# The experts' tiles written out for TensorE, both passes in one block, and semaphores cleared by ranges

## What is computed

```python
x = x + _L0_xattn_ref(_layernorm(x, axis=-1), ctx_1024, ctx_1024)
x = x + _L0_ffn_ref(_layernorm(x, axis=-1), L0_ffn_gate_w, L0_ffn_w_gate, L0_ffn_w_up, L0_ffn_w_down)
x = x + _L1_xattn_ref(_layernorm(x, axis=-1), ctx_1024, L1_xattn_Wq, L1_xattn_Wk, L1_xattn_Wv, L1_xattn_Wo)
x = x + _L1_ffn_ref(_layernorm(x, axis=-1), ...)

# _L0_ffn_ref
topk_w, topk_ids = jax.lax.top_k(scores, TOP_K)          # 8 of 64 experts a token
topk_w = topk_w / (topk_w.sum(axis=-1, keepdims=True) + 1e-20)
sorted_tokens = x[sort_idx // TOP_K]
g = jax.lax.ragged_dot(sorted_tokens, jnp.swapaxes(w_gate, 1, 2), group_sizes)
u = jax.lax.ragged_dot(sorted_tokens, jnp.swapaxes(w_up, 1, 2), group_sizes)
h = jax.nn.silu(g) * u
out = jax.lax.ragged_dot(h, jnp.swapaxes(w_down, 1, 2), group_sizes)
y = (unsorted.reshape(B * S, TOP_K, D) * topk_w[..., None]).sum(axis=1)
```

## Time and profile before

| | us |
|---|---|
| median of 3 runs | 1179.89 (1178.31 to 1189.08) |
| profiled execution | 1183.53 |
| its span, first to last instruction | 1181.7 |
| TensorE busy in the span | 934.0 (79%) |
| VectorE, GpSimd, ScalarE busy | 614.7, 535.2, 360.8 |

### The profile page before, as it was taken

How to read it: one execution, slowest core, us unless ns; L and a number is a source line. 1 busy time by engine, 2 the same in 40 slices (tenths; PEclk the granted TensorE clock), 3 DMA queues, 4 the chain that set the end, 5 groups by cost and what they waited for, 6 DMA issues and landing times. The chain is left out here.

```text
span 1181.7 us, 22184 instructions
## 1 busy us (share of the span) xinstructions
PE 934.0 (79%) x5670; PEld 627.6 (53%) x5671; DVE 614.7 (52%) x1818; ACT 360.8 (31%) x884; POOL 535.2 (45%) x514
## 2 busy tenths in 40 slices
PE   1178778765499999999899999803788886799999
PEld 1035454454266666666666666502566664465665
DVE  6568988874144444444444444436878772333230
ACT  3426555613122222222222222111255564122211
POOL 4400776776476677676677667413253200000000
PEclk9999888988699999999999999955799999699999
DMA  6464534015455565555656666252877541100000
GB/s 221 156 161 126 112 87 101 24 32 170 139 188 187 160 206 186 179 183 176 194 186 207 206 199 205 78 218 70 251 193 213 147 105 30 58 9 10 18 18 19
DMA packets 78846, 160.39 MB, mean 136 GB/s; under 512 B 18448, under 2 KB 44048, under 8 KB 76480
## 3 DMA queue, kind: packets, MB, share of 16 engines
q1 hardware_dynamic: 59264, 112.23, 32.3%
q0 software_dynamic: 19520, 47.41, 13.0%
HBM read 118.09 MB, written 41.22 MB: 135 GB/s over the span
## 5 line engine op out<-in xcount | busy, mean ns | idle before, releaser
L1279 PE MATMUL ex_ps<-ex_w_gu,ex_rows_t 128*128 x640 | 263.1, 493 | 27.5 <-issue 17.0
L1248 POOL DMA_INDIRECT expert_outs<-ex_result,slot_places x160 | 157.4, 984 | 102.5 <-DVE ex_result L1391 101.6
L1243 POOL DMA_INDIRECT ex_rows<-moe_rows,slot_tokens x160 | 153.9, 962 | 57.7 <-issue 48.8
L881 POOL DMA_INDIRECT expert_lists<-rt_number,rt_idx x128 | 123.9, 968 | 105.8 <-DVE rt_idx L988 63.7
L1298 PE MATMUL ex_ps<-ex_w_down,ex_hidden_t 96*128 x640 | 166.8, 382 | 1.0 <-DVE ex_hidden_t L1383 1.0
L616 ACT ACTIVATE a_probs<-a_ps 128x512 f32<-128x512 f32 (+1 forms) x256 | 133.2, 541 | 96.3 <-PE a_ps L478 48.1
L1353 ACT ACTIVATE ex_act_g<-ex_ps 128x192 f32<-128x192 f32 x160 | 52.9, 330 | 353.3 <-PE ex_ps L1279 353.3
L461 PE MATMUL a_ps<-stacked_keys,a_qst 96*128 96x256 bf16 (+1 forms) x512 | 109.6, 287 | 56.4 <-DMA stacked_keys<-k_stack 26.7
L1279 PEld LDWEIGHTS ex_ps<-ex_w_gu,ex_rows_t 128*128 128x128 f32 x640 | 108.4, 192 | 43.2 <-issue 36.0
L1391 DVE TENSOR_SCALAR ex_result<-ex_ps,ex_rows 128x256 f32<-128x256 f32 x160 | 77.4, 484 | 93.5 <-PE ex_ps L1298 93.5
L1298 PEld LDWEIGHTS ex_ps<-ex_w_down,ex_hidden_t 96*128 96x128 f32 x640 | 108.3, 189 | 13.1 <-issue 2.4
(11 more groups left out here) (222 smaller groups left out, 1408.7 us busy)
## 6 DMA issues: line engine op xcount, KB each, us to landing
ex_w_gu<-in_w_gu_dram SPq DMA_DIRECT2D x64, 384.0 KB, 3.3
cb_gathered<-expert_outs SPq DMA_DIRECT2D x16, 1024.0 KB, 5.6
ex_w_down<-in_w_down_dram SPq DMA_DIRECT2D x64, 192.0 KB, 3.9
a_qst<-q_stack SPq DMA_DIRECT2D x32, 192.0 KB, 4.0
stacked_keys<-k_stack SPq DMA_DIRECT2D x32, 192.0 KB, 4.1
a_qst<-q_stack SPq DMA_DIRECT2D x32, 128.0 KB, 3.8
stacked_keys<-k_stack SPq DMA_DIRECT2D x32, 128.0 KB, 4.0
k_stack<-split_parts SPq DMA_DIRECT2D x8, 384.0 KB, 2.6
```

The lines of the kernel that those rows point to most:

```text
L881: nc.gpsimd.indirect_dma_start(k.lists, bass.IndirectOffsetOnAxis(ap=self.idx[:, t, s:s + 1], axis=0), self.number[:, t, s:s + 1], None).t ...
L1243: nc.gpsimd.indirect_dma_start(rows[:, t % R, :], None, k.xn.rearrange("t p d -> (t p) d"), bass.IndirectOffsetOnAxis(ap=k.ids[:, begin + ...
L1248: nc.gpsimd.indirect_dma_start(k.outs, bass.IndirectOffsetOnAxis(ap=k.places[:, begin + t:begin + t + 1], axis=0), result[:, t % R], None) ...
L1279: last = pe.matmul(ps[:, 2 + j % 2, 0:2 * FF], rows_t[:, j % 2, c * P:(c + 1) * P], w_gu[:, bass.ds(ring, 1), c, :].rearrange("p a n -> p ...
```

## The change

- experts() is called once. Both passes are in one block and share the tiles in SBUF and PSUM; each pass has semaphores of its own, and the second pass first waits for the first one's placements. One block and one sweep fewer.
- TensorE's 20 rounds are all written out (the second pass's 4 as well), and the kind of the next tile is loaded in every tile, also in the last of a round, and carried on.
- SyncE waits at the end of a pass for the placements, and issues the first four row loads of attention a1 (load_expert_rows) before the experts' block ends. The tile gathered and its two semaphores are made before the experts.
- A sweep clears each run of neighbouring semaphores with one instruction.

```diff
         @block.sync
         def _(sp):
-            for sem in used:
-                sp.sem_clear(sem)
+            left = sorted(sem.num for sem in used)
+            while left:
+                n = 1
+                while n < len(left) and left[n] == left[0] + n:
+                    n += 1
+                sp.sem_clear(range(left[0], left[0] + n))
+                left = left[n:]
...
+def load_expert_rows(eng, k, t, u, j):
+    rows = k.outs[bass.ds(t * P * TOP_K, P * TOP_K)].rearrange("(p s) d -> p (s d)", s=TOP_K)
+    eng.dma_start(k.gathered[:, u, j].rearrange("p s d -> p (s d)"), rows).then_inc(k.rows_in[u], 16)
+
+
+def experts(nc, k):
...
-        w_in = [sem(f"w_in{j}") for j in range(WRING)]
-        weights_ready = sem("weights_ready")
-        KINDS = min(EXPERTS, end - begin)
...
-        result_ready = sem("result_ready")
-        placed = [k.indirect(f"{tag}_placed{j}") for j in range(R)]
-        ROUNDS = (end - begin) // R
-        table = k.table[:, :, begin:end]
...
+        def semaphores(n):
+            one = Kernel()
+            one.w_in = [sem(f"w_in{j}_{n}") for j in range(WRING)]
+            one.rows_in = [k.indirect(f"ex{n}_rows_in{j}") for j in range(R)]
+            one.placed = [k.indirect(f"ex{n}_placed{j}") for j in range(R)]
+            one.weights_ready = sem(f"weights_ready{n}")
+            one.rows_turned, one.rows_copied = sem(f"rows_turned{n}"), sem(f"rows_copied{n}")
...
+            one.result_ready = sem(f"result_ready{n}")
+            return one
+
+        passes = [(0, EXPECTED, semaphores(0)), (EXPECTED, ETILES, semaphores(1))]
...
+        @contextmanager
+        def needed(eng, begin):
             if begin == 0:
-                return nullcontext()
-            return eng.If(eng.value_load(k.tiles_used[0:1, 0:1], min_val=1, max_val=ETILES) > begin)
+                yield
+            else:
+                with eng.If(eng.value_load(k.tiles_used[0:1, 0:1], min_val=1, max_val=ETILES) > begin):
+                    for j in range(R):
+                        eng.wait_ge(passes[0][2].placed[j], 16 * (begin // R))
+                    yield
...
+                for begin, end, one in passes:
+                    ROUNDS, table = (end - begin) // R, k.table[:, :, begin:end]
+                    KINDS = min(EXPERTS, end - begin)
...
+                    with needed(sp, begin):
+                        base = 0 if begin == 0 else sp.value_load(k.first_kind[0:1, 0:1], min_val=0, max_val=EXPERTS - 1)
                         for j in range(WRING):
-                            load(base, i, j)
-                            publish(*((i, j - AHEAD) if j >= AHEAD else (i - 1, j - AHEAD + WRING)))
-                    for j in range(WRING - AHEAD, WRING):
-                        publish(KINDS // WRING - 1, j)
+                            load(base, 0, j)
+                            if j >= AHEAD:
+                                publish(0, j - AHEAD)
+                        with sp.Fori(1, KINDS // WRING) as i:
+                            for j in range(WRING):
+                                load(base, i, j)
+                                publish(*((i, j - AHEAD) if j >= AHEAD else (i - 1, j - AHEAD + WRING)))
+                        for j in range(WRING - AHEAD, WRING):
+                            publish(KINDS // WRING - 1, j)
+                        for j in range(R):
+                            sp.wait_ge(one.placed[j], 16 * ROUNDS)
+                for t in range(4):
+                    load_expert_rows(sp, k, t, t // 2, t % 2)
...
-                    following = kind_of(*after(i, j, 1)) if left > 1 and j < R - 1 else None
...
-                def steps(i, last=False):
-                    kinds = (None, kind_of(i, 0))
-                    if not isinstance(i, int) or i:
-                        kinds = (kind_of(i - 1, R - 1), kinds[1])
-                    for j in range(R):
-                        kinds = step(i, j, kinds, first=(isinstance(i, int) and i == j == 0), left=R - j if last else R)
-
-                with needed(pe):
-                    pe.sem_inc(down_ready, begin + 1)
-                    turn_rows(0, 0)
-                    turn_rows(0, 1)
-                    steps(0)
-                    with pe.Fori(1, ROUNDS - 1) as i:
-                        steps(i)
-                    steps(ROUNDS - 1, last=True)
-                    turn_hidden(ROUNDS - 1, R - 1)
-                    down(ROUNDS - 1, R - 1, kind_of(ROUNDS - 1, R - 1))
...
+                    def step(i, j, kinds, first=False, left=R):
+
+                        before = (i, j - 1) if j else (i - 1, R - 1)
+                        gate_up(i, j, kinds[1], 0)
+                        if not first:
+                            turn_hidden(*before)
+                        gate_up(i, j, kinds[1], 1)
+                        following = kind_of(*after(i, j, 1)) if left > 1 else None
+                        if left > 2:
+                            turn_rows(*after(i, j, 2))
+                        if not first:
+                            down(*before, kinds[0])
+                        return kinds[1], following
+
+                    def steps(i, kinds, last=False):
+                        for j in range(R):
+                            kinds = step(i, j, kinds, first=(i == j == 0), left=R - j if last else R)
+                        return kinds
+
+                    with needed(pe, begin):
+                        pe.sem_inc(one.down_ready, begin + 1)
+                        turn_rows(0, 0)
+                        turn_rows(0, 1)
+                        kinds = (None, kind_of(0, 0))
+                        for i in range(ROUNDS):
+                            kinds = steps(i, kinds, last=(i == ROUNDS - 1))
+                        turn_hidden(ROUNDS - 1, R - 1)
+                        down(ROUNDS - 1, R - 1, kinds[0])
...
-        self.gathered = sb("gathered", [P, 2, 2, TOP_K, D], F32)
+        self.gathered = k.gathered
...
-        self.rows_in = [sem("rows_in0"), sem("rows_in1")]
+        self.rows_in = k.rows_in
...
-        rows = self.k.outs[bass.ds((4 * i + 2 * u + j) * P * TOP_K, P * TOP_K)].rearrange("(p s) d -> p (s d)", s=TOP_K)
-        sp.dma_start(self.gathered[:, u, j].rearrange("p s d -> p (s d)"), rows).then_inc(self.rows_in[u], 16)
+        load_expert_rows(sp, self.k, 4 * i + 2 * u + j, u, j)
 
     def sync_first(self, sp, load):
-        for u in range(2):
-            for j in range(2):
-                self.load_rows(sp, 0, u, j)
         sp.dma_start(self.wq[:], self.k.dram["wq"]).then_inc(self.w_in, 16)
         for j in range(2):
...
-        experts(nc, k, 0, EXPECTED)
-        experts(nc, k, EXPECTED, ETILES)
-        attention(nc, k, "a1", k.q1_stack, k.k1_stack, k.v1, 1.0 / float(np.sqrt(np.float32(DH))), True, k.ao, Combine())
+        with ExitStack() as late:
+            k.gathered = late.enter_context(nc.sbuf_tensor("gathered", [P, 2, 2, TOP_K, D], F32))
+            k.rows_in = [late.enter_context(nc.semaphore(f"combine_rows_in{u}")) for u in range(2)]
+            experts(nc, k)
+            attention(nc, k, "a1", k.q1_stack, k.k1_stack, k.v1, 1.0 / float(np.sqrt(np.float32(DH))), True, k.ao, Combine())
```

287 lines of the change are left out of this document (136 added, 151 removed).

## The result

The changed kernel took 1143.02 us (median of four runs, 1136.69 to 1144.32), the kernel before in the same rounds 1184.49 us (four runs, 1178.31 to 1193.07). The ratio is 0.9643 with a 95% interval from 0.959 to 0.9696. In later rounds it was 1136.76 us (six runs, 1131.03 to 1142.79) against 1185.79, ratio 0.9594 [0.9552, 0.9635]. The prediction was 1135 us, a gain of 45.4 us. The medians show gains of 41.5 and 49.0 us.

The account below looks back on a forecast made before the run. TensorE's matmuls were taken as the bound within expert rounds, its own instruction stream between them. 34.5 - 1.9 + 7.9 + 4.9 = 45.4 us took the median from 1179.9 to 1134.5, given as 1135, range 1123 to 1153.

Parts of the forecast that it names:

- The boundary: Between expert rounds: removing TensorE's stall gains 1.81 us at each of 19 boundaries, 34.5 us; VectorE's loop gives back 1.9.
- GpSimd: In expert rounds: its 2.56 us a tile stays under TensorE's 2.60, so 0 cost; bad end 8 us.
- instruction fetch: In the written-out rounds: 18 or 19 new code fetches on TensorE's queue cost 0.
- rival 1: In expert rounds: TensorE stops at each fetched block; 1209 us (slower, 0.04), mild form 1158 (0.05 together with a remaining stall).
- rival 2: In expert rounds: GpSimd becomes the bound, 0.05 us a tile over TensorE's, 8 us back, 1143 us; chance 0.06.
- The sweeps: Semaphore clears between blocks: merging neighbours shortens three sweeps by 2.1, 3.6 and 2.2 us, together 7.9 us.
- The way to the second attention: Between experts and second attention: SyncE's early issue starts the row loads at 775.1 instead of 780.05, gaining 4.9 us.
- rival 3: Before the second attention: SyncE's jump over the second pass is short, loads 3.8 us earlier still, 1131 us; chance 0.06.
- this would be hidden: At the experts' end: TensorE's 3.9 us branch over the unused pass would be over before the last placement completes.
- medians would follow the profiled execution: Whole kernel: the runs' median stays 3.6 us below the profiled execution, 1138.1, so becomes 1134.5.
- Rival 4: Last stage: a pause shorter by 2.2 us may keep TensorE's clock up, saving 5 to 8 us, about 1128; chance 0.05.
- The median of before: Whole kernel: the starting median was taken as 1179.9 us, from which the forecast gain led to 1134.5.

Follow-up runs that it names:

- experiment 1: Kernel before with only TensorE's rounds written out and each tile's kind loaded one tile ahead; two passes, single clears and late row loads kept: 1154.31 us, ratio 0.9767.
- experiment 3: Changed kernel with TensorE's hardware loop and its two kind loads at each round's start put back: 1173.49 us, ratio 0.9891.
- experiment 4: Changed kernel with TensorE written out without a loop, but two kind loads at each round's start as before: 1157.54 us, ratio 0.9786.
- experiment 9: Changed kernel with VectorE's rounds written out too, in place of its hardware loop: 1133.32 us, ratio 0.9571.
- experiment 6: Changed kernel with each semaphore cleared by its own instruction again, in all four sweeps: 1142.42 us, ratio 0.9673.
- experiment 8: Changed kernel with single clears instead of range clears, and each semaphore cleared twice: 1149.14 us, ratio 0.9725.
- experiment 5: Changed kernel with the first row loads issued at the start of SyncE's attention program again, after block end and clears: 1144.29 us, ratio 0.9639.
- experiment 2: Kernel before with only the semaphore clears merged into ranges: 1173.53 us, ratio 0.9919.
- Experiment 7: Changed kernel run again without any edit, giving its second trace: 1136.76 us, ratio 0.9594.
- experiment 10: Changed kernel with 36 matmuls whose results nobody reads added on TensorE ahead of the last stage: 1132.74 us, ratio 0.9551.
- experiment 11: Changed kernel with both VectorE's rounds written out and 36 unread matmuls ahead of the last stage: 1129.14 us, ratio 0.9531.
- experiment 12: Kernel of experiment 11 with 140 more unread matmuls at the second attention's start and 40 at the experts' start: 1139.92 us, ratio 0.9626.

## Why the prediction was right, step by step

**The boundary, 34.5 less 1.9 us: right.** 32.6 us were forecast, 33.27 measured (32.3 in the second trace, whose first round is longer). The round went from 22.59 to 20.86 us, 1.73 a boundary against 1.71 (1.81 less 0.10). Experiments 1 and 3 show that it all comes from TensorE's program, 4 one way in which it splits between loop and loads, and 9 that what is left over the 20.78 us of eight tiles is VectorE's loop, 0.09 us.

**GpSimd and instruction fetch, 0 each: right.** Rivals 1 and 2 didn't come. There were 19 more fetches, as counted, and TensorE works in 83.44 of 83.44 us. Late in the rounds GpSimd still starts a placement 0.30 us after VectorE's result and is named as waiting for it; over the whole kernel that is so for 124 of the 160:

```profile
702.95 0.99 POOL L1273 DMA_INDIRECT expert_outs<-ex_result,slot_places  x1 [0.30 <-DVE ex_result L1419]
...
POOL expert_outs L1273 <- DVE ex_result L1419: 58.0, 124, 4.3
```

Its two transfers and their gaps are still 2.56 us a tile, so this margin stayed as thin as the prediction had it.

**The sweeps, 7.9 us: right**, 7.6 in the trace (2.18, 3.45, 1.98 for 2.1, 3.6, 2.2). A clear of a range took 0.03 to 0.10 us, however many semaphores it covered (up to 64 in two). Experiments 6 and 8 show the pauses as the price of single clears.

**The way to the second attention, 4.9 us: undersized.** This is the step of the prediction that was off: "by the 4.7 us with its test, about 3.8" for SyncE's jump. The jump was short, 0.5 us to the next instruction, as rival 3 had it with a chance of 0.06. The loads start 8.24 us earlier, and 7.6 arrive at the first sum (8.1 in the second trace). By experiment 5, 2.8 to 3.3 us are due to the loads' new place. The rest is left for the merged block and the shorter jump together; no run parts the two. A short jump of SyncE alone would have brought little: in experiment 2 it was short as well, but the block waited for TensorE's branch, and the loads came 1.5 us earlier. In the merged block TensorE passes its branch of 3.5 us before the last placement has landed; that this would be hidden was right. In experiment 1, with both blocks and single clears as before, SyncE's jump was in between (branch at 747.8, drain at 750.1); what decides its length was not isolated.

**Not in the sum: the granted clock.** The first stage lost 5.1 us and the last 2.2 in the profiled run. Experiment 7 shows the first to be scatter, and the last as well: the same program of that stage took 179.9 us in experiments 5 and 9. The forecast that medians would follow the profiled execution was therefore good to some 6 us only: in the second set of rounds the changed kernel was at 1136.8. The parts of the sum gained 48.5 us in the trace (33.27, 7.6 and 7.6) and the stages' scatter took 7.9 back; that the total of 40.8 us comes so near to 45.4 is partly luck. Rival 4 had the mechanism (the clock falls around TensorE's pauses, shown by 10) but a wrong trigger: shortening the pause from 3.70 to 1.72 us did not keep the clock up; its low pieces there were 27.4 us before and 34.1 or 20.5 behind the shorter pause. Filling the pause did.

**The median of before** was 1184.5 us in the rounds of the comparison, not 1179.9; with that the forecast gain stood for 1139.

## What to carry to other kernels

Where a pipelined engine stands still at regular distances, look at its sequencer: loads of registers, loop counts and branches that nothing covers at a loop's edge. Issue the load an iteration ahead across the edge, which here brought 18.3 us behind the 14.5 of the branch's removal, and then look for the next engine's loop, since each costs a little too. Merge semaphore clears between stages, and put the first loads of the next stage in front of the barrier. Read gains under 1% from the traces, stage by stage, and double a suspected cost when its removal is lost in the scatter.

## What was not expected of the hardware

- One kernel's first attention took 242.7 us in one run and 250.7 in another, at mean granted clocks of 0.92 and 0.87.
- The same kind of jump over the unused pass takes 3.4 to 4.3 us on TensorE in every trace, but on SyncE 3.8, 2.3 or 0.5 us. The Trainium skill (Runtime: NRT & Kernel Launch, Instruction fetch mechanics) says that a branch out of the fetched window must wait for the target; the long ones fit this, no run here varies the distance alone.
- GpSimd's drain behind its last indirect DMA takes 2.24 us, with all placements already landed, and holds the block's end (experiment 5).
- Nineteen more code blocks of some 16 KB each (0.80 MB in 49) were fetched beside full TensorE work without a gap. VectorE's rounds written out brought 12 more on q14 (42 for 30), and no round became longer by them.
- With 36 matmuls that compute nothing ahead of it the last stage took 176.3, 176.7 and 178.4 us (experiments 10, 11 and 12), without them 179.6 to 183.6 (the changed kernel twice, and 5, 6 and 9).
